# Item records loaded and added inside the aggregation stage, in four column chunks

## The chip, the cores and the metric

The kernel runs on one core of one Trainium2 chip. Its engines are TensorE (PE, matrix products), VectorE (DVE), ScalarE (ACT), GpSimd (POOL) and SyncE (SP), beside 16 DMA engines. Each engine has its own instruction stream; streams meet only at semaphores. The metric is the time of one execution on the device, in microseconds.

## The reference, cut to what matters

Four layers run one after the other over a graph of 6250 nodes with 256 features and 200,000 edges. The first is a weighted aggregation; it is the one that the change touches:

```
y   = layernorm(x)
x   = x + segment_sum(edge_weight[:, None] * y[dst], src)     # 200,000 edges
x   = x + experts(layernorm(x))
x   = x + graph_attention(layernorm(x), src, dst)
x   = x + lstm_layer(layernorm(x))                            # 6250 steps
```

## The kernel before

The nodes are cut into 49 blocks of 128. The edges are sorted by the block of their source node into "items": one item is a column of 128 edges that all belong to one block, and two neighbouring items always belong to the same block. There is room for 1664 items. The stages run one behind the other; each is a block of the program that every engine must leave before the next one starts:

- **stage_scatter** (L161) computes a place for every edge and writes a record of three floats (source, destination, weight; 12 bytes) with one indirect DMA for each 128 edges into tables in device memory. There are five such tables (`WAYS`), so that five scatters can be under way; a place holds its record in one table and zeros in the other four. The stage also stores the normalised rows y in device memory, and makes `BW` (the block of each item).
- **stage_items** (L430) loads the five tables, 128 partitions by 1664 items by 3 floats each, adds them up on VectorE, and takes the sum apart into `DST` (the node to gather, an integer), `EW` (the weight) and `LO` (the source's position in its block). `BI` holds the block number of each pair of items.
- **stage_aggregate** (L491) has 104 turns of 16 items. ScalarE copies a half turn's eight columns of `DST` to `ag_idx`; GpSimd issues one indirect DMA per item that gathers 128 rows of y (1 KB each); VectorE makes a 128x128 matrix per item ("pick": the weight where a column number equals `LO`, else zero); TensorE multiplies pick by rows and sums each pair of items; VectorE adds the pair's sum to its block of `X`. There is one set of 16 row buffers. Four of them are refilled together: in turn i GpSimd waits, ahead of its gathers 4q to 4q+3, until the pairs 2q and 2q+1 of turn i-1 have been summed (`summed`), and for the index copy (`staged`).
- then the experts, the attention (which uses `DST`, `LO` and `EW` again) and the LSTM, each behind the one before.

Constants: P = 128, NI = 1664, U = 16, UP = 8, RF = 3, WAYS = 5, TURNS = 104. On VectorE, `link(...)` issues an instruction and then waits for its end.

Of the kernel before, what the change touches and what calls it, by code (L numbers as in the profile page):

```python
# [16 lines left out]
ALU = mybir.AluOpType  # L17
# [4 lines left out]
P = 128  # L22
# [3 lines left out]
NB = -(-N // P)  # L26
# [11 lines left out]
U = 16  # L38
# [3 lines left out]
UP = U // 2  # L42
NI = -(-((E - NB) // (2 * P) + NB) // UP) * U
TURNS = NI // U
RF = 3
SU = 20
WAYS = 5
# [19 lines left out]
def pair_blocks(nc, g, engine, i, k0, n):  # L67

    return nc.values_load_multi_w_load_instructions(
        g["BI"][0:1, ds(i * UP + k0, n)], [engine], min_val=0, max_val=NB,  # L70
        skip_runtime_bounds_check_because="a number of blocks counted on the chip, at most NB")[1]
# [356 lines left out]


def stage_items(nc, sb, sem, g):  # L430
    part = [sb(f"rec_part{k}", [P, NI * RF]) for k in range(WAYS)]
    loaded, step = sem("rec_loaded"), sem("items_step")
    with nc.Block() as block:
        @block.sync
        def _(sp):
            for k in range(WAYS):
                sp.dma_start(part[k][:, :], g["rec"][k].rearrange("(p r) f -> p (r f)", p=P)).then_inc(loaded, 16)

        @block.vector
        def _(dve):  # L440
            n = [0]

            def link(ins):
                n[0] += 1
                ins.then_inc(step, 1)
                dve.wait_ge(step, n[0])

            dve.wait_ge(loaded, 16 * WAYS)

            for k in range(1, WAYS):  # L450
                link(nc.vector.tensor_tensor(part[0][:, :], part[0][:, :], part[k][:, :], ALU.add))
            rec = part[0][:, :].rearrange("p (r f) -> p r f", f=RF)
            link(nc.vector.tensor_copy(g["DST"][:, 0:NI], rec[:, :, 1]))
            link(nc.vector.tensor_copy(g["EW"][:, 0:NI], rec[:, :, 2]))

            link(nc.vector.tensor_scalar(part[1][:, 0:NI], g["BW"][:, :], float(P), 1.0, ALU.mult, ALU.add))
            link(nc.vector.tensor_tensor(g["LO"][:, 0:NI], rec[:, :, 0], part[1][:, 0:NI], ALU.subtract))

            link(nc.vector.tensor_copy(g["BI"][0:1, 0:NI // 2], g["BW"][0:1, 0:NI:2]))

            link(nc.vector.memset(g["BI"][0:1, NI // 2:NI // 2 + UP], NB))
            link(nc.vector.memset(g["DST"][:, NI:NI + U], 0))
            link(nc.vector.memset(g["LO"][:, NI:NI + U], -1.0))
            link(nc.vector.memset(g["EW"][:, NI:NI + U], 0.0))


def gather_rows(pool, nc, g, table, rows, idx, staged, summed):

    with pool.Fori(0, TURNS) as i:
        for q in range(GPT):  # L470
            if q % 2 == 0:
                pool.wait_ge(staged, i * 2 + (q // 2 + 1))
            pool.wait_ge(summed, i * UP + 2 * (q + 1))
            own_wait(pool, g)
            for u in range(q * GU, (q + 1) * GU):
                pool.indirect_dma_start(rows[:, u, :], None, table,  # L476
                                        bass.IndirectOffsetOnAxis(ap=idx[:, u // HU, u % HU:u % HU + 1], axis=0)).then_inc(g["got"][q], 16)


def stage_indices(nc, g, idx, i, h, staged):  # L480
    nc.scalar.copy(idx[:, h, :], g["DST"][:, ds(i * U + h * HU, HU)]).then_inc(staged, 1)
# [9 lines left out]
def stage_aggregate(nc, sb, sem, g):  # L491
    idx = sb("ag_idx", [P, 2, HU], I32)
    rows = sb("ag_rows", [P, U, D])
    pick = sb("ag_pick", [P, U, P])
    free = sb("ag_free", [1, 2])
    sums = [g["ps"][k][:, 0:D] for k in range(UP)]
    staged, picked, summed, added = (sem(n) for n in ("ag_staged", "ag_picked", "ag_summed", "ag_added"))
    with nc.Block() as block:
        @block.scalar
        def _(act):  # L500
            for h in range(2):
                stage_indices(nc, g, idx, 0, h, staged)
            with act.Fori(0, TURNS) as i:
                for h in range(2):
                    for q in (2 * h, 2 * h + 1):
                        act.wait_ge(g["got"][q], i * (16 * GU) + 16 * GU)
                    stage_indices(nc, g, idx, i + 1, h, staged)

        @block.gpsimd
        def _(pool):  # L510
            pool.memset(free[:, 0:1], 0.0).then_inc(summed, UP)
            gather_rows(pool, nc, g, g["y"], rows, idx, staged, summed)

        @block.tensor
        def _(pe):
            with pe.Fori(0, TURNS) as i:
                for k in range(UP):
                    pe.wait_ge(picked, i * UP + (k + 1))
                    pe.wait_ge(added, i * UP + (k + 1))
                    if k % 2 == 0:  # L520
                        pe.wait_ge(g["got"][k // 2], i * (16 * GU) + 16 * GU)
                    for u in (2 * k, 2 * k + 1):
                        m = nc.tensor.matmul(sums[k], pick[:, u, :], rows[:, u, :], start=u == 2 * k, stop=u == 2 * k + 1)  # L523
                    m.then_inc(summed, 1)

        @block.vector
        def _(dve):
            def picks(i, h):
                dve.wait_ge(summed, i * UP + (h + 1) * (UP // 2))
                for u in range(h * HU, (h + 1) * HU):  # L530
                    m = nc.vector.tensor_scalar(pick[:, u, :], g["iota"][:, :], g["LO"][:, ds(i * U + u, 1)], g["EW"][:, ds(i * U + u, 1)],
                                                ALU.is_equal, ALU.mult)
                    if u % 2 == 1:
                        m.then_inc(picked, 1)

            def adds(i, h):
                blocks = pair_blocks(nc, g, mybir.EngineType.DVE, i, h * UP // 2, UP // 2)
                for n, b in enumerate(blocks):
                    k = h * UP // 2 + n
                    dve.wait_ge(summed, i * UP + (UP + k + 1))  # L540
                    dve.wait_ge(added, i * UP + (UP + k))
                    nc.vector.tensor_tensor(g["X"][:, ds(b, 1), :], g["X"][:, ds(b, 1), :], sums[k], ALU.add).then_inc(added, 1)

            nc.vector.memset(free[:, 1:2], 0.0).then_inc(added, UP)
            picks(0, 0)
            with dve.Fori(0, TURNS) as i:
                picks(i, 1)
                adds(i, 0)
                picks(i + 1, 0)
                adds(i, 1)  # L550
# [1164 lines left out]
def build(nc, ins, out):  # L1715
    with ExitStack() as ctx:
# [24 lines left out]
        with ExitStack() as items:  # L1741
            kept = lambda name, shape, dt=F32: items.enter_context(nc.sbuf_tensor(name, shape, dt))
            g["BW"] = kept("item_block", [P, NI])
            g["BI"] = kept("pair_block", [1, NI // 2 + UP], I32)
            with ExitStack() as recs:
                g["REC"] = recs.enter_context(nc.sbuf_tensor("records", [EP, EC, RF], F32))
                g["POS"] = recs.enter_context(nc.sbuf_tensor("places", [EP, EC], I32))
                stage(stage_places)
                stage(stage_scatter)
            g["DST"] = kept("item_dst", [P, NI + U], I32)  # L1750
            g["LO"] = kept("item_lo", [P, NI + U])
            g["EW"] = kept("item_weight", [P, NI + U])
            stage(stage_items)
            stage(stage_aggregate)
            stage(stage_experts)
            g["AS"] = kept("alpha_src_and_max", [P, NB + 1, 2 * HEADS])
            stage(stage_heads)
            g["NUM"] = kept("numerators", [P, NB + 1, D + HEADS])
            with ExitStack() as scores:
                g["ADE"] = scores.enter_context(nc.sbuf_tensor("item_alpha_dst", [P, NI + U, HEADS], F32))  # L1760
                stage(stage_maxima)
                stage(stage_attend)
            stage(stage_project)
# [16 lines left out]
```

## Time and profile before

| | us |
|---|---|
| median of 3 runs (22097.25 to 22099.84) | 22098.49 |
| profiled execution, its time | 22100.69 |
| profiled execution, span of the trace | 22099.0 |
| last scatter of stage_scatter starts | 2162.64 |
| loads of stage_items are issued from | 2168.74 |
| first gather of stage_aggregate | 2231.95 |
| last gather of stage_aggregate starts | 4340.13 |
| next stage (experts) begins | about 4361 |

Times in the trace count from the start of the span. The span runs from the first to the last instruction, so it is 1.7 us short of the execution's own time. The work around the change fills 0.06 ms of 22 ms; about three fifths of the span are the LSTM's.

### The profile page before, as it was taken

The page shows a single profiled execution, that of the slowest core. Times are in us where ns is not written, and L with a number is a line of the kernel's source. Part 1 is how long each engine was busy: PE and PEld are TensorE (multiplying, and loading weights), DVE is VectorE, ACT ScalarE, POOL GpSimd, SP SyncE. Part 2 cuts the span into 40 slices and gives each one's busy share as a digit, 9 for nine tenths or more (in the row PEclk, how much of TensorE's full clock was granted, in tenths as well). Part 3 has the DMA queues.
Part 4 walks back from the last instruction along what each step waited for, and adds up shares of the span by engine and source line. Part 5 has one row for each costly group of instructions (what it writes and reads, how often), then busy time and mean ns, then how long its engine had stood idle before and what let it go on. Part 6 is the DMA issues. An engine that isn't in the chain of part 4 may idle for free. (4 is left out here: it accounts for less than half of the span.)

```text
span 22099.0 us, 1508424 instructions
## 1 busy us (share of the span) xinstructions
PE 17428.3 (79%) x637604; PEld 12607.9 (57%) x637604; DVE 11072.8 (50%) x43264; ACT 7724.9 (35%) x35209; POOL 6178.2 (28%) x11376
## 2 busy tenths in 40 slices
PE   0000555577888888999999999999999999999998
PEld 0000333355666665666666666666666666666665
DVE  6500333336666666555555555555555555555555
ACT  1000000025555553444444444444444444444443
POOL 6776777605444442000000000000000000000000
PEclk9999777787777778999999999999999999999999
DMA  1001333402222223000000000000000000000000
GB/s 40 1 1 36 99 104 104 88 12 68 63 64 64 64 64 82 2 2 2 2 2 2 2 2 2 2 2 2 2 2 2 2 2 2 2 2 2 2 2 13
DMA packets 334772, 559.74 MB, mean 25 GB/s; under 512 B 141918, under 2 KB 219138, under 8 KB 333314
## 3 DMA queue, kind: packets, MB, share of 16 engines
q0 software_dynamic: 210480, 460.22, 7.8%
q1 hardware_dynamic: 124242, 98.95, 1.4%
q8 instruction: 19, 0.31, 0.0%
q14 instruction: 31, 0.25, 0.0%
HBM read 498.35 MB, written 60.37 MB: 25 GB/s over the span
## 5 line engine op out<-in xcount | busy, mean ns | idle before, releaser
L1468 PE MATMUL banks<-ls_wake 128*1 128x512 bf16 x65000 | 5779.7, 379 | 0.0
L1462 POOL TENSOR_TENSOR ls_d<-ls_sf,ls_cell 128x2 f32<-128x2 f32 x6250 | 1256.1, 201 | 11880.2 <-ACT ls_sf L1523 11880.2
L1507 PE MATMUL banks<-ls_w,ls_ht 128*2 128x64 f32 x200000 | 3937.2, 219 | 1.2 <-issue 1.2
L523 PE MATMUL banks<-ag_rows,ag_pick 128*128 128x256 f32 x3328 | 1207.9, 527 | 3080.6 <-DMA ag_rows<-y_table,ag_idx 3053.9
L1523 ACT ACTIVATE ls_sf<-ls_f_cols 128x2 f32<-128x2 f32 x6250 | 1278.3, 205 | 5636.3 <-DVE ls_f_cols L1559 5636.3
L1559 DVE STREAM_TRANSPOSE ls_f_cols<-banks 128x64 f32<-128x64 f32 x6250 | 1559.8, 250 | 3289.3 <-PE banks L1501 3289.3
L1507 PEld LDWEIGHTS banks<-ls_w,ls_ht 128*2 128x2 f32 x200000 | 3099.5, 85 | 1.3 <-issue 1.3
L523 PEld LDWEIGHTS banks<-ag_rows,ag_pick 128*128 128x128 f32 x3328 | 836.4, 263 | 3451.5 <-DMA ag_rows<-y_table,ag_idx 2432.9
L1501 PE MATMUL banks<-ls_w,ls_ht 128*1 128x64 f32 x100000 | 2525.5, 218 | 323.8 <-issue 0.5
L1501 PEld LDWEIGHTS banks<-ls_w,ls_ht 128*1 128x1 f32 x100000 | 1352.4, 82 | 2295.4 <-DVE ls_ht L1571 2294.7
L1512 PE MATMUL banks<-ls_w,ls_ht 128*1 128x64 f32 x100000 | 2541.3, 219 | 1.0 <-issue 1.0
L998 POOL DMA_INDIRECT at_rows<-row_table,at_idx x1664 | 1659.6, 997 | 1869.5 <-ACT at_idx L1010 1399.8
L1561 DVE STREAM_TRANSPOSE ls_ig_cols<-banks 128x64 f32<-128x64 f32 x6250 | 1558.4, 249 | 1235.0 <-PE banks L1507 1235.0
L1480 PE MATMUL banks<-ls_xp,ls_sel 128*1 128x64 f32 x50000 | 1840.2, 219 | 261.3 <-DVE ls_ig_cols L1561 249.9
L1571 DVE SCALAR_TENSOR_TENSOR ls_ht<-ls_to,ls_tc 128x2 f32<-128x2 f32 x6250 | 1015.9, 163 | 1692.7 <-ACT ls_tc L1530 1692.7
L1491 PE MATMUL banks<-ls_xp,ls_sel 128*1 128x64 f32 x50000 | 1844.0, 219 | 0.0
L1485 PE MATMUL banks<-ls_xp,ls_sel 128*2 128x64 f32 x50000 | 1834.4, 218 | 0.0
L1525 ACT ACTIVATE ls_d<-ls_ig_cols 128x4 f32<-128x4 f32 x6250 | 1302.7, 208 | 1515.3 <-DVE ls_ig_cols L1561 1515.3
L259 POOL DMA_INDIRECT rec_table<-st_rec,st_idx x1560 | 1586.4, 1017 | 548.0 <-issue 472.4
L476 POOL DMA_INDIRECT ag_rows<-y_table,ag_idx x1664 | 1594.7, 958 | 515.6 <-issue 495.3
L1512 PEld LDWEIGHTS banks<-ls_w,ls_ht 128*1 128x1 f32 x100000 | 1697.3, 84 | 1.2 <-issue 1.2
L1468 PEld LDWEIGHTS banks<-ls_wake 128*1 128x1 bf16 x65000 | 1684.4, 84 | 0.0
(324 smaller groups left out, 22962.4 us busy)
## 6 DMA issues: line engine op xcount, KB each, us to landing
ag_rows<-y_table,ag_idx POOLq DMA_INDIRECT x1664
at_rows<-row_table,at_idx POOLq DMA_INDIRECT x1664
projections<-xp_out SPq DMA_DIRECT2D x49, 512.0 KB, 2.6
rec_table<-st_rec,st_idx POOLq DMA_INDIRECT x1563, 2.1
ls_xp<-projections SPq DMA_DIRECT2D x1250, 12.0 KB
ls_xp<-projections SPq DMA_DIRECT2D x1250, 8.0 KB, 1.5
rec_table<-zero POOLq DMA_DIRECT2D x5, 2496.0 KB, 18.3
rec_part<-rec_table SPq DMA_DIRECT2D x5, 2496.0 KB, 19.9
```

The lines of the kernel that those rows point to most:

```text
L259: pool.indirect_dma_start(g["rec"][k], bass.IndirectOffsetOnAxis(ap=idx[:, h, u % SH:u % SH + 1], axis=0), recs[:, h, u % SH, :], None).th ...
L476: pool.indirect_dma_start(rows[:, u, :], None, table, bass.IndirectOffsetOnAxis(ap=idx[:, u // HU, u % HU:u % HU + 1], axis=0)).then_inc(g ...
L523: m = nc.tensor.matmul(sums[k], pick[:, u, :], rows[:, u, :], start=u == 2 * k, stop=u == 2 * k + 1)
L998: pool.indirect_dma_start(rows[:, r, u, :], None, g["rows"], bass.IndirectOffsetOnAxis(ap=idx[:, r, u:u + 1], axis=0)).then_inc(g["got"][r ...
L1468: nc.tensor.matmul(bank_wake[32 * j:32 * j + 1, :], wake[:, 0:1], wake[:, :], start=True, stop=True, tile_position=(0, 32 * j))
L1480: nc.tensor.matmul(bank_f[32 * j:32 * j + 1, 0:HD], sel[:, u, j, 0:1], xp[:, b, HD:2 * HD], start=True, stop=False, tile_position=(0, 32 * j))
L1485: nc.tensor.matmul(bank_ig[32 * j:32 * j + 2, 0:HD], sel[:, u, j, :], xp[:, b, 0:HD], start=True, stop=False, tile_position=(0, 32 * j))
L1491: x = nc.tensor.matmul(bank_o[32 * j:32 * j + 1, 0:HD], sel[:, u, j, 1:2], xp[:, b, HD:2 * HD], start=True, stop=False, tile_position=(0, ...
L1501: m = nc.tensor.matmul(bank_f[32 * j:32 * j + 1, 0:HD], ht[:, v, c, 1:2], w[:, c, j, HD:2 * HD], start=False, stop=c == 1, tile_position=( ...
L1507: m = nc.tensor.matmul(bank_ig[32 * j:32 * j + 2, 0:HD], ht[:, v, c, 1 - r:3 - r], w[:, c, j, lo:lo + HD], start=False, stop=(r, c) == (1, ...
L1512: m = nc.tensor.matmul(bank_o[32 * j:32 * j + 1, 0:HD], ht[:, v, c, 1:2], w[:, c, j, 3 * HD:4 * HD], start=False, stop=c == 1, tile_positi ...
L1559: vec.transpose(f_cols[:, :], bank_f[:, 0:HD]).then_inc(turned, 1)
```

## The change

stage_items is emptied. Its loads and its arithmetic move into stage_aggregate, cut into `COLS` = 4 chunks of `CI` = 416 items:

- SP issues 20 loads instead of 5: for each chunk the same 416 columns of all five tables, 128 rows of 4,992 bytes each, with one semaphore per chunk. The tiles have the same bytes as before; their shape is written with three dimensions.
- VectorE first scales `BW` (now into `EW`, which serves as scratch for it) and makes `BI`, then for each chunk waits for its five loads, does the four additions, the copy to `DST` (which raises `known`), the subtraction to `LO` and the copy to `EW`. The padding of the three tiles comes last; that of `DST` raises `known` a fifth time. Only behind all this stand the picks of turn 0 and the loop.
- ScalarE waits for `known` 1 before the index copies of turn 0, and for `known` 5 before its loop, which copies the indices of turn 1 and later.

GpSimd's and TensorE's programs are the same as before.

```diff
--- before.py
+++ after.py
@@ -428,40 +428,9 @@
 
 
 def stage_items(nc, sb, sem, g):
-    part = [sb(f"rec_part{k}", [P, NI * RF]) for k in range(WAYS)]
-    loaded, step = sem("rec_loaded"), sem("items_step")
-    with nc.Block() as block:
-        @block.sync
-        def _(sp):
-            for k in range(WAYS):
-                sp.dma_start(part[k][:, :], g["rec"][k].rearrange("(p r) f -> p (r f)", p=P)).then_inc(loaded, 16)
-
-        @block.vector
-        def _(dve):
-            n = [0]
-
-            def link(ins):
-                n[0] += 1
-                ins.then_inc(step, 1)
-                dve.wait_ge(step, n[0])
-
-            dve.wait_ge(loaded, 16 * WAYS)
-
-            for k in range(1, WAYS):
-                link(nc.vector.tensor_tensor(part[0][:, :], part[0][:, :], part[k][:, :], ALU.add))
-            rec = part[0][:, :].rearrange("p (r f) -> p r f", f=RF)
-            link(nc.vector.tensor_copy(g["DST"][:, 0:NI], rec[:, :, 1]))
-            link(nc.vector.tensor_copy(g["EW"][:, 0:NI], rec[:, :, 2]))
-
-            link(nc.vector.tensor_scalar(part[1][:, 0:NI], g["BW"][:, :], float(P), 1.0, ALU.mult, ALU.add))
-            link(nc.vector.tensor_tensor(g["LO"][:, 0:NI], rec[:, :, 0], part[1][:, 0:NI], ALU.subtract))
-
-            link(nc.vector.tensor_copy(g["BI"][0:1, 0:NI // 2], g["BW"][0:1, 0:NI:2]))
-
-            link(nc.vector.memset(g["BI"][0:1, NI // 2:NI // 2 + UP], NB))
-            link(nc.vector.memset(g["DST"][:, NI:NI + U], 0))
-            link(nc.vector.memset(g["LO"][:, NI:NI + U], -1.0))
-            link(nc.vector.memset(g["EW"][:, NI:NI + U], 0.0))
+
+    g["columns"] = 4
+
 
 
 def gather_rows(pool, nc, g, table, rows, idx, staged, summed):
@@ -493,13 +462,25 @@
     rows = sb("ag_rows", [P, U, D])
     pick = sb("ag_pick", [P, U, P])
     free = sb("ag_free", [1, 2])
+    COLS = g["columns"]
+    CI = NI // COLS
+    part = [sb(f"rec_part{k}", [P, NI, RF]) for k in range(WAYS)]
+    loaded, step, known = [sem(f"rec_loaded{c}") for c in range(COLS)], sem("items_step"), sem("items_known")
     sums = [g["ps"][k][:, 0:D] for k in range(UP)]
     staged, picked, summed, added = (sem(n) for n in ("ag_staged", "ag_picked", "ag_summed", "ag_added"))
     with nc.Block() as block:
+        @block.sync
+        def _(sp):
+            for c in range(COLS):
+                for k in range(WAYS):
+                    sp.dma_start(part[k][:, c * CI:(c + 1) * CI, :], g["rec"][k].rearrange("(p r) f -> p r f", p=P)[:, c * CI:(c + 1) * CI, :]).then_inc(loaded[c], 16)
+
         @block.scalar
         def _(act):
+            act.wait_ge(known, 1)
             for h in range(2):
                 stage_indices(nc, g, idx, 0, h, staged)
+            act.wait_ge(known, COLS + 1)
             with act.Fori(0, TURNS) as i:
                 for h in range(2):
                     for q in (2 * h, 2 * h + 1):
@@ -541,7 +522,28 @@
                     dve.wait_ge(added, i * UP + (UP + k))
                     nc.vector.tensor_tensor(g["X"][:, ds(b, 1), :], g["X"][:, ds(b, 1), :], sums[k], ALU.add).then_inc(added, 1)
 
+            n = [0]
+
+            def link(ins):
+                n[0] += 1
+                ins.then_inc(step, 1)
+                dve.wait_ge(step, n[0])
+
             nc.vector.memset(free[:, 1:2], 0.0).then_inc(added, UP)
+            link(nc.vector.tensor_scalar(g["EW"][:, 0:NI], g["BW"][:, :], float(P), 1.0, ALU.mult, ALU.add))
+            link(nc.vector.tensor_copy(g["BI"][0:1, 0:NI // 2], g["BW"][0:1, 0:NI:2]))
+            link(nc.vector.memset(g["BI"][0:1, NI // 2:NI // 2 + UP], NB))
+            for c in range(COLS):
+                cols = slice(c * CI, (c + 1) * CI)
+                dve.wait_ge(loaded[c], 16 * WAYS)
+                for k in range(1, WAYS):
+                    link(nc.vector.tensor_tensor(part[0][:, cols, :], part[0][:, cols, :], part[k][:, cols, :], ALU.add))
+                nc.vector.tensor_copy(g["DST"][:, cols], part[0][:, cols, 1]).then_inc(known, 1)
+                link(nc.vector.tensor_tensor(g["LO"][:, cols], part[0][:, cols, 0], g["EW"][:, cols], ALU.subtract))
+                link(nc.vector.tensor_copy(g["EW"][:, cols], part[0][:, cols, 2]))
+            nc.vector.memset(g["DST"][:, NI:NI + U], 0).then_inc(known, 1)
+            link(nc.vector.memset(g["LO"][:, NI:NI + U], -1.0))
+            link(nc.vector.memset(g["EW"][:, NI:NI + U], 0.0))
             picks(0, 0)
             with dve.Fori(0, TURNS) as i:
                 picks(i, 1)
```

## Rows read from the trace of the kernel before

**Rows 1.** Busy time by stretch: stretch, its length, engines, PEclk, DMA share, GB/s.

```profile
2184.00:2188.00 4.00, 0.00 (x0) 0.00 (x0) 0.00 (x0) 0.00 (x0) 0.00 (x0) 1.00 1.00 429
2500.00:3900.00 1400.00, 800.02 (x2216) 553.44 (x2216) 523.06 (x1666) 27.25 (x138) 1062.46 (x1109) 0.76 0.35 104
4300.00:4340.00 40.00, 20.97 (x48) 15.07 (x48) 11.17 (x36) 0.59 (x3) 24.38 (x26) 0.74 0.95 78
```

**Rows 2.** Timeline, 2160 to 2253 us: start, length, engine, line, operation, idle before.

```profile
2162.64 0.91 POOL L266 DMA_INDIRECT rec_table<-st_rec,st_idx  x1 [0.30 <-issue]
2168.74 2.41 SPq L437 DMA_DIRECT2D rec_part<-rec_table  x5
2201.44 21.54 DVE L451 TENSOR_TENSOR rec_part<-rec_part 128x4992 f32<-128x4992 f32 x4 [453.12 <-DMA rec_part<-rec_table]
2223.01 1.27 DVE L453 CAST item_dst<-rec_part 128x1664 int32<-128x1664 f32 x1
...
2225.62 1.03 DVE L456 TENSOR_SCALAR rec_part<-item_block 128x1664 f32<-128x1664 f32 x1
2226.68 2.37 DVE L457 TENSOR_TENSOR item_lo<-rec_part 128x1664 f32<-128x1664 f32 x1
2229.09 0.58 DVE L459 CAST pair_block<-item_block 1x832 int32<-1x832 f32 x1
...
2230.74 0.30 ACT L481 COPY ag_idx<-item_dst 128x8 int32<-128x8 int32 x2 [82.17 <-PEq L433]
...
2230.85 4.26 DVE L531 TENSOR_SCALAR ag_pick<-iota,item_lo,item_weight 128x128 f32<-128x128 f32 x16
2231.95 1.01 POOL L476 DMA_INDIRECT ag_rows<-y_table,ag_idx  x1 [1.14 <-ACT ag_idx L481]
...
2238.58 3.78 PE L523 MATMUL banks<-ag_rows,ag_pick 128*128 128x256 f32 x8 [2167.45 <-DMA ag_rows<-y_table,ag_idx]
...
2242.51 0.42 DVE L542 TENSOR_TENSOR X<-X,banks 128x256 f32 x1 [1.28 <-PE banks L523]
...
2252.25 0.96 POOL L476 DMA_INDIRECT ag_rows<-y_table,ag_idx  x1 [0.30 <-issue]
```

**Rows 3.** All gathers of L476: duration ns min/median/max, and idle before them.

```profile
L476 POOL DMA_INDIRECT ag_rows<-y_table,ag_idx x1664: 950/957/1077, 2231.9 to 4340.1; - x185
...
  issue: 495.3, 1626
```

**Rows 4.** All instructions on the tile rec_part: the loads, and their landing.

```profile
L437 SPq DMA_DIRECT2D rec_part<-rec_table x5: 349/426/543, 2168.7 to 2170.7; - x5
...
DMA to landing us min/median/max: 8.9/19.9/30.8
```

**Rows 5.** Shorter VectorE additions (L542, L1215): duration ns min/median/max.

```profile
L542 DVE TENSOR_TENSOR X<-X,banks x832: 404/421/423, 2240.8 to 4359.7; 128x256 f32 x167
...
L1215 DVE TENSOR_TENSOR at_msg<-at_rows,at_msg x104: 679/681/684, 5080.0 to 8589.5; 128x512 f32<-128x512 f32 x104
```

**Rows 6.** Busy time by stretch, columns as in group 1.

```profile
4.00:10.00 6.00, 0.00 (x0) 0.00 (x0) 0.00 (x0) 0.00 (x0) 5.82 (x9) 1.00 0.93 349
2000.00:2100.00 100.00, 0.00 (x0) 0.00 (x0) 0.00 (x0) 2.78 (x16) 76.16 (x79) 1.00 0.02 1
```

**Rows 7.** Timeline where indirect DMAs meet VectorE operations with two SBUF inputs.

```profile
800.98 1.95 DVE L392 SCALAR_TENSOR_TENSOR item_block<-item,cum,item_block 128x1664 f32<-128x1664 f32 x1 [0.41 <-DVE item_block L392]
801.72 2.05 POOL L259 DMA_INDIRECT rec_table<-st_rec,st_idx  x1 [0.30 <-issue]
803.33 1.95 DVE L392 SCALAR_TENSOR_TENSOR item_block<-item,cum,item_block 128x1664 f32<-128x1664 f32 x1 [0.41 <-DVE item_block L392]
...
5080.03 0.68 DVE L1215 TENSOR_TENSOR at_msg<-at_rows,at_msg 128x512 f32<-128x512 f32 x1
...
5080.55 1.00 POOL L998 DMA_INDIRECT at_rows<-row_table,at_idx  x1 [0.30 <-issue]
5080.63 0.42 DVE L1223 TENSOR_TENSOR numerators<-numerators,at_fade 128x260 f32 x1
```

## The prediction

> **What bounds the kernel now.** I first looked at the busy times of the page and at its slices, to see how much work can be touched at all, then at the timeline between the last scatter and the second turn of the aggregation, then at the lines of the gathers and of the loads. The reader should see three things.
>
> First, the stretch from 2168.74 to 2231.95 us, 63.2 us, is one serial chain [rows 2]. SP issues five loads; VectorE, idle until then, starts its additions at 2201.44; four additions take 21.54 us, and the copies, the scaling, the subtraction and `BI` follow until about 2230.2; then a stage border, the index copy at 2230.74, and the first gather at 2231.95. Nothing else runs beside it. The loads run at full rate: 429 GB/s at a DMA share of 1.00 [rows 1].
>
> Second, the aggregation is bound by GpSimd's issue of gathers. 1664 of them take 957 ns in the median, and nearly all of the idle time before them (495.3 us, 0.30 us for each) ended by "issue", that is by nothing that the trace shows to be waited for [rows 3]. One gather costs 1.27 us and a turn of 16 costs 20.3 (2231.95 to 2252.25) [rows 2]. TensorE is busy 57% and VectorE 37% of a middle stretch, DMA 0.35 at 104 GB/s [rows 1]. In the last turns the DMA engines bind (0.95 at 78 GB/s) [rows 1]; those turns also hang on the turn before, so they move with the rest. So an earlier gather 17, the first of turn 1, is an earlier end of the stage by the same amount, provided that GpSimd then runs on without a pause. The next stages begin only behind this one.
>
> Third, therefore the right quantity is the start of gather 17, now 2252.25 us, and not that of gather 1: turn 0 has its row buffers free and needs only `known` 1, but turn 1 needs turn 0 summed, and for that the picks, which need all four chunks.
>
> **The change, step by step.** The last scatter, the border behind it and SP's first issue stay: 2168.7 us.
>
> *The load of a chunk.* A table's load was 2.556 MB. The first landed 8.9 us after its issue and the last, issued at 2170.7, after 30.8 [rows 4], so at 2201.5. At 429 GB/s 2.556 MB are 5.96 us, which leaves 3.0 us ahead of the first. A chunk is a quarter of each of the five tables, 5 x 0.639 = 3.195 MB, 7.45 us at 429. Its pieces are 4,992 bytes instead of 19,968, and the trace has no such load. The nearest row is the load of the edges in pieces of 6,248 bytes, 349 GB/s [rows 6]. I take 400, between the two, because that row also holds the start and the end of its transfers: 8.0 us a chunk, bounds 7.45 and 9.15. Twenty issues at 0.48 us (2.41 for five) [rows 2] end 9.7 us after the first and hold nothing up. So chunk 0 is there at 2168.7 + 3.0 + 8.0 = 2179.7.
>
> *VectorE's work on a chunk.* L1215 takes 681 ns for 512 columns and L542 421 ns for 256 [rows 5]; from 512 to 4992 columns (5.36 us [rows 2]) the slope is 1.044 ns, so about 0.15 us of each instruction is fixed. Four additions of 1248 columns: 4 x (0.15 + 1.30) and 0.16 of gaps, 5.96 us. `DST` costs (1.27 - 0.15) / 4 + 0.15 = 0.43 and `EW`, the same copy of a column in three, as much, `LO` (2.37 - 0.15) / 4 + 0.15 = 0.71 [rows 2]; with the gaps 7.6 us a chunk, 30.4 in all, against 26.4 for the same work before (21.54 + 2 x 1.27 + 2.37). The scaling of `BW` and the copy to `BI`, 1.03 and 0.58 us [rows 2], now lie ahead of the wait for chunk 0, hidden by its load; without that cover they would cost 1.6.
>
> *Gather 1.* 2179.7 + 6.0 + 0.45 = 2186.2 for `known` 1. From the index copy to the gather it was 1.2 us (2230.74 to 2231.95) [rows 2]: 2187.4, which is 44.5 us earlier than before. Turn 0 ends 20.3 us later, at 2207.7.
>
> *The chunks behind it.* Chunk 1 lands at 2187.7 and is done at 2195.3. Chunks 2 and 3 share the DMA engines with the gathers of turn 0. By bytes the gathers take 104 of 429 GB/s, a quarter; by their DMA share they take 0.35 [rows 1]. I take the bytes, since shares of two queues may overlap. Chunk 2 lands at 2188.5 + 7.2 / 0.76 = 2198.0 and is done at 2205.6; chunk 3 lands at 2208.5 and is done at 2216.1. So the load and not VectorE ends last.
>
> *Gather 17.* Behind chunk 3 stand the padding (0.3), the first two picks (4.26 / 16 each, 0.5) [rows 2], and two pairs on TensorE: from 2238.58 to VectorE's addition at 2242.51 it was 3.9 us [rows 2]. With 0.3 for the semaphores gather 17 starts 5.0 us behind 2216.1, at 2221.1. The index copy of turn 1, queued on ScalarE behind `known` 5, is ready some 3 us earlier. The wait for `known` 5 thus costs nothing of its own: ScalarE has nothing else, and the picks hold turn 1 longer. After it, the next pairs take 3.8 us for two [rows 2], GpSimd 5.1 for four gathers, so it doesn't pause again.
>
> *Sum.* 2252.25 - 2221.1 = 31 us less. The border between the two stages (0.6 us) is in it. Against the profiled execution's own 22100.7 us that gives 22069.7; against the median, which is 2.2 us lower, 22067.5.
>
> *A lock that the trace shows.* While VectorE runs an operation with two SBUF inputs, an indirect DMA of GpSimd does not end: beside additions of 1.95 us (L392) it takes 2.05 us instead of 0.96, and it ends 0.84 us behind each of them; the same at 5080.55, where L1215 ends at 5080.71 and the DMA at 5081.55 [rows 7]. The change puts twelve such additions (chunks 1 to 3) beside turn 0. One gather for each addition makes 1.49 us a gather, at most 24 us for turn 0, which then ends at 2211, still ahead of gather 17. I cost it at nothing, with the ten microseconds until 2221 as the cover. The Trainium skill has this as a rule (SBUF - State Buffer, "Who interferes with whom": whichever of the two starts first holds the shared port pair for its whole instruction); by the rows it holds here, though the page infers that `tensor_tensor` spares the making of descriptors, and by that turn 0 would end at 2207.7: the sum is 31 us either way.
>
> **The rivals.**
>
> *VectorE is the bound.* If the gathers take nothing from the loads, chunk 3 lands at 2203.7 and VectorE ends at 2179.7 + 30.4 = 2210.1; gather 17 at 2215.1, 37 us less, 22061. At 429 GB/s as well 22060.5. For it: gathers are small beside the loads. Against: the loads already fill the DMA engines (share 1.00) [rows 1].
>
> *Slow loads.* With 349 GB/s [rows 6] and 0.35 of the engines lost to gathers, chunk 0 lands at 2180.9, chunk 2 at 2204.0, chunk 3 at 2214.8; gather 17 at 2227.5, 25 us less, 22074.
>
> *The lock holds through all additions.* If GpSimd gets in only between chunks and not between additions, turn 0 grows by 3 x 6.0 us and ends at 2225.6: 27 us less, 22072. Against it: the DMA at 5080.55 was let in at 5080.71 although the next operation with two SBUF inputs stood directly behind (5080.63) [rows 7].
>
> *Every load pays its start.* If the 20 loads ran one behind the other with 3.0 us each, a chunk would take 5 x 4.5 = 22.3 us and chunk 3 would land near 2258; gather 17 at 2271, 18 us more, 22117. Against it: the five loads now landed 5.9 us apart, all of it transfer [rows 4]. The Trainium skill speaks for a part of it (DMA: Bandwidth & Descriptors, "Rules for kernel authors": at least 1 MiB for each DMA for full rate; the loads shrink from 2.4 to 0.6 MiB); its figure of 341 GB/s at 1 MB gives about what "Slow loads" gives from rows.
>
> *The loads fall into records; this is the other side.* The tile and the table are now written with the record's 3 floats as a dimension of their own. If the transfer is cut along it, it has 1.06 million pieces of 12 bytes instead of 2,560. The scatters move such pieces: 79 of them, 10,112 pieces, for a share of 0.02 of 16 engines over 100 us [rows 6], 3.2 ns of an engine a piece. That makes 213 us for the loads instead of 32, so chunk 3 comes some 175 us later: 22098 - 31 + 175, about 22243, and several times as much if a piece costs more from device memory. The change is slower as soon as the load takes 31 us more than I think. Against it: in each row the columns of a chunk are contiguous on both sides, and the whole-table transfer was not cut.
>
> **How the numbers follow.** My forecast of 31 us, with the load as the last to end, has 0.50; VectorE as the bound 0.22; slow loads 0.10; the lock through all additions 0.05; a start for every load 0.03; records 0.05; something that I don't see 0.05. The likeliest time is 22067.5. The range for 8 in 10 takes in the first four cases with 2 to 4 us at either end for the fixed costs: 22057 to 22080. A measurement tells this kernel from no change at about 0.2%, 44 us. The gain can't pass that: gather 17 can't start before turn 0's 16 gathers are issued, 44.5 us earlier than now, and VectorE's 30.4 us keep it 7 us behind that. So faster by over 0.2% has 0.04 (a part of what I don't see, above all a later stage that runs otherwise), within 0.2% 0.89, slower 0.07 (the records, and 0.02 of what I don't see).
>
> **What the changed profile would show.** SP issues 20 loads from about 2168.7; the first addition starts at 2179.7; gather 1 at 2187 and gather 17 at 2221; between them gathers that end 0.84 us behind an addition; VectorE idle before the additions of chunks 2 and 3 with the load as releaser; the experts 31 us earlier, all later stages shifted by the same. The prediction is wrong if gather 17 is released by something else than TensorE, if the number of packets of SP's queue grows by far more than 2,160, or if a later stage lasts otherwise than before.

## The result and the profile after

| | before | changed |
|---|---|---|
| median of 22 runs, us | 22098.47 (22094.49 to 22101.55) | 22068.14 (22062.24 to 22072.14) |
| ratio of the changed kernel to before, 95% interval | | 0.9986 [0.998, 0.9992] |
| span of the profiled execution, us | 22099.0 | 22066.8 |

The change takes 30.3 us off, 0.14%; 31 had been forecast, at 22067.5 us. All 22 runs of one kernel lie apart from all 22 of the other. One of the ten runs of e6_psum_adds below took 32339.5 us at a mean granted clock of 0.618, where all other runs in this text have 0.915 to 0.928, and it is left out.

The page of the changed kernel gives the span, SP's queue (packets, MB, share of the DMA engines) and the gathers of the aggregation (now L445; busy, mean ns, idle before):

```profile
span 22066.8 us, 1508142 instructions
...
q1 hardware_dynamic: 126402, 98.96, 1.4%
...
L445 POOL DMA_INDIRECT ag_rows<-y_table,ag_idx x1664 | 1599.9, 961 | 539.1 <-issue 498.7
```

SP's queue had 124,242 packets before. It has 2,160 more, which is 15 more transfers of 144 packets each: the chunks' rows are moved whole, and the 3 floats of a record were not cut apart.

The timeline of the changed kernel over the same stretch as [rows 2]:

```profile
2161.97 0.91 POOL L266 DMA_INDIRECT rec_table<-st_rec,st_idx  x1 [0.30 <-issue]
2168.06 16.77 SPq L476 DMA_DIRECT2D rec_part<-rec_table  x20
...
2168.14 1.03 DVE L533 TENSOR_SCALAR item_weight<-item_block 128x1664 f32<-128x1664 f32 x1
...
2178.55 5.93 DVE L540 TENSOR_TENSOR rec_part<-rec_part 128x1248 f32<-128x1248 f32 x4 [8.64 <-DMA rec_part<-rec_table]
2184.52 0.44 DVE L541 CAST item_dst<-rec_part 128x416 int32<-128x416 f32 x1
...
2184.99 0.30 ACT L450 COPY ag_idx<-item_dst 128x8 int32<-128x8 int32 x2 [37.08 <-DVE item_dst L541]
...
2186.10 5.93 DVE L540 TENSOR_TENSOR rec_part<-rec_part 128x1248 f32<-128x1248 f32 x4
2186.20 2.24 POOL L445 DMA_INDIRECT ag_rows<-y_table,ag_idx  x1 [18.04 <-ACT ag_idx L450]
2188.75 1.14 POOL L445 DMA_INDIRECT ag_rows<-y_table,ag_idx  x1 [0.30 <-issue]
...
2194.43 0.96 POOL L445 DMA_INDIRECT ag_rows<-y_table,ag_idx  x1 [0.30 <-issue]
2194.75 5.93 DVE L540 TENSOR_TENSOR rec_part<-rec_part 128x1248 f32<-128x1248 f32 x4 [1.11 <-DMA rec_part<-rec_table]
...
2205.11 5.93 DVE L540 TENSOR_TENSOR rec_part<-rec_part 128x1248 f32<-128x1248 f32 x4 [2.82 <-DMA rec_part<-rec_table]
...
2209.19 1.19 POOL L445 DMA_INDIRECT ag_rows<-y_table,ag_idx  x1 [0.30 <-issue]
2211.07 0.44 DVE L541 CAST item_dst<-rec_part 128x416 int32<-128x416 f32 x1
...
2212.16 0.43 DVE L543 COPY item_weight<-rec_part 128x416 f32<-128x416 f32 x1
2212.66 0.07 DVE L544 MEMSET item_dst<- 128x16 int32 x1
...
2212.94 4.19 DVE L512 TENSOR_SCALAR ag_pick<-iota,item_lo,item_weight 128x128 f32<-128x128 f32 x16
2213.07 0.38 ACT L450 COPY ag_idx<-item_dst 128x8 int32 x2 [27.79 <-DVE item_dst L544]
...
2213.68 9.80 PE L504 MATMUL banks<-ag_rows,ag_pick 128*128 128x256 f32 x32 [2142.54 <-DVE ag_pick L512]
...
2218.26 0.95 POOL L445 DMA_INDIRECT ag_rows<-y_table,ag_idx  x1 [7.89 <-PE banks L504]
...
2219.52 0.95 POOL L445 DMA_INDIRECT ag_rows<-y_table,ag_idx  x1 [0.30 <-issue]
```

What the reader is to see: SP issues 20 loads from 2168.06. VectorE's first additions start at 2178.55, not at 2201.44. ScalarE copies the first indices at 2184.99, and gather 1 starts at 2186.20 instead of 2231.95 [rows 2]. The additions of chunks 2 and 3 stand behind a wait for their loads (1.11 and 2.82 us). GpSimd has issued the 16 gathers of turn 0 by 2210.38 and then waits 7.89 us for TensorE, whose wait ended with the picks (L512), which in turn stand behind the last chunk. Gather 17 starts at 2218.26; before it started at 2252.25, without a wait [rows 2].

The loads beside nothing and beside gathers, by stretch (columns as in [rows 1]), and the loads and their landing:

```profile
2172.00:2184.00 12.00, 0.00 (x0) 0.00 (x0) 5.35 (x4) 0.00 (x0) 0.00 (x0) 1.00 1.02 416
2188.00:2204.00 16.00, 0.00 (x0) 0.00 (x0) 12.86 (x13) 0.00 (x0) 12.65 (x12) 1.00 1.02 401
```

```profile
L476 SPq DMA_DIRECT2D rec_part<-rec_table x20: 350/487/3072, 2168.1 to 2183.5; - x20
...
DMA to landing us min/median/max: 4.1/13.8/21.5
```

All 16 DMA engines stay full in both stretches. SP's issues grow to 3.07 us at most, but the last load is issued at 2183.5, 21 us ahead of its landing, so the issue holds nothing up.

**Where the time went.** The executions place the whole stretch differently: SP's first load is at 2168.7 us before and at 2168.1 and 2165.4 in two executions of the changed kernel. In the rest of the text I count from that issue. Gather 17 stands at 83.5 us before and at 50.2 now, 33.3 less; the next stage begins (first load of the experts) at 2192.1 before and 2159.1 now, 33.1 less; the spans differ by 32.2 and the medians by 30.3. So the stage passes its gain on whole.

### The profile page after: what moved, and what is told of

It is laid out like the page before. It is cut to its first block and busy times, and to the rows that moved or that the text cites. A ratio compares the mean times of both kernels' runs of the same rounds, so it can differ in the third digit from the quotient of the medians.

```text
span 22066.8 us, 1508142 instructions
## 1 busy us (share of the span) xinstructions
PE 17362.8 (79%) x637293; PEld 12587.0 (57%) x637604; DVE 11073.9 (50%) x43285; ACT 7726.5 (35%) x35209; POOL 6175.0 (28%) x11376
## 5 line engine op out<-in xcount | busy, mean ns | idle before, releaser
L445 POOL DMA_INDIRECT ag_rows<-y_table,ag_idx x1664 | 1599.9, 961 | 539.1 <-issue 498.7
```

Of the source, the lines that this page charges most:

```text
L445: pool.indirect_dma_start(rows[:, u, :], None, table, bass.IndirectOffsetOnAxis(ap=idx[:, u // HU, u % HU:u % HU + 1], axis=0)).then_inc(g ...
```

## The experiments

Two groups of four ran on one chip each, and each kernel is compared with the kernel before on the same chip (median 22092.91 us in the first group, 22097.29 in the second). All columns but the last count from SP's first load in the profiled execution; the last is the median of before less that of the kernel, with the ratio's 95% interval.

| kernel | gather 1 | gather 17 | experts begin | less than before |
|---|---|---|---|---|
| before | 63.2 | 83.5 | 2192.1 | |
| changed, 22 runs | 18.1 | 50.2 | 2159.1 | 30.3 [0.998, 0.9992] |
| e1_gathers_last | 42.4 | 62.6 | 2167.2 | 19.7 [0.9983, 1.0001] |
| e2_early_picks | 18.0 | 41.3 | 2148.0 | 41.4 [0.9973, 0.9991] |
| e3_one_chunk | 56.9 | 78.7 | 2183.8 | 6.4 [0.9988, 1.0006] |
| e4_eight_chunks | 11.9 | 50.3 | 2156.9 | 30.0 [0.9978, 0.9996] |
| e5_two_chunks | 30.9 | 58.4 | 2161.8 | 26.7 [0.9979, 0.9997] |
| e6_psum_adds | 18.0 | 50.1 | 2155.3 | 31.1 [0.9976, 0.9996] |
| e7_interleaved | 6.3 | 29.9 | 2137.4 | 49.9 [0.9968, 0.9986] |
| e8_changed_again | 17.9 | 50.0 | 2155.5 | 30.8 [0.9977, 0.9995] |

The intervals of the two groups are about 0.09% wide to each side, 20 us, so e1 and e3 can't be told from the kernel before by them alone. What tells these kernels apart is the place of gather 17 in the trace: how much earlier than before's it is agrees with the last column to within 4 us in every row.

### e1_gathers_last: the loads and VectorE overlap, the gathers don't

```diff
-            act.wait_ge(known, 1)
+            act.wait_ge(known, COLS + 1)
             for h in range(2):
                 stage_indices(nc, g, idx, 0, h, staged)
```

> Four chunks as in the changed kernel, but ScalarE waits for all chunks before it copies the indices of turn 0, so no gather runs beside loads or chunk work. Theory (the first gather of turn 1, gather 17, sets the end; loads are slowed by gathers): without gathers beside them the loads no longer hold VectorE up, its chunk work ends at about 2209.2 (2178.5 + 4 x 7.56 + 0.4) instead of 2212.9, gather 1 starts at 2210.5 and gather 17 20.3 us later at 2230.8, 12.5 us behind the changed kernel's 2218.3: about 22080.5. Rival (the gain is all from overlapping loads with VectorE, turn 0 is no part of it): no change from 22068.

Measured: gather 17 12.6 us behind e8's, 19.7 us less than before instead of 18 forecast. The rival falls: the gathers of turn 0 are part of the gain. The timeline shows the additions of chunks 2 and 3, the padding of `DST` and gather 1:

```profile
2190.68 5.94 DVE L540 TENSOR_TENSOR rec_part<-rec_part 128x1248 f32<-128x1248 f32 x4 [0.39 <-DMA rec_part<-rec_table]
...
2198.21 5.93 DVE L540 TENSOR_TENSOR rec_part<-rec_part 128x1248 f32<-128x1248 f32 x4
...
2205.77 0.07 DVE L544 MEMSET item_dst<- 128x16 int32 x1
...
2207.09 1.01 POOL L445 DMA_INDIRECT ag_rows<-y_table,ag_idx  x1 [42.24 <-ACT ag_idx L450]
```

SP's first issue is at 2164.74 here. Behind chunk 0 only chunk 2 is waited for (0.39 us), 25.9 us behind that issue, and chunk 3 is there in time: VectorE sets the end of the chunk work. With gathers beside it (changed kernel) the last additions began 37.1 us behind the issue, here 33.5: the gathers beside the loads cost 3.6 us, where the expectation had 3.7.

### e2_early_picks: turn 0's picks behind chunk 0

```diff
             for c in range(COLS):
...
                 link(nc.vector.tensor_copy(g["EW"][:, cols], part[0][:, cols, 2]))
+                if c == 0:
+                    picks(0, 0)
+                    picks(0, 1)
...
-            picks(0, 0)
-            with dve.Fori(0, TURNS) as i:
+            adds(0, 0)
+            picks(1, 0)
+            adds(0, 1)
+            with dve.Fori(1, TURNS) as i:
                 picks(i, 1)
```

ScalarE copies the indices of turn 1 ahead of its wait for all chunks, too.

> The picks of turn 0 stand directly behind chunk 0, and ScalarE copies the indices of turn 1 before it waits for all chunks. Theory: gather 17 is then released by gather 16 and not by TensorE behind the last chunk; turn 0 takes about 24 us from 2186.2 because of the lock, so gather 17 starts at 2210.5, 8 us earlier than in the changed kernel: about 22060. Rival A (something other than the picks behind the last chunk holds gather 17, or GpSimd pauses at turn 2 instead): 22068. Rival B (without the lock turn 0 would take 20.3 us): gather 17 at 2206.8, 22056.5.

Measured: gather 17 stands at 41.3 us, 8.7 earlier than in e8 (8 forecast), and the median is 41.4 us under before's. The timeline shows the picks, the first matrix products, gathers 16 and 17 and the end of the chunk work:

```profile
2183.55 4.32 DVE L516 TENSOR_SCALAR ag_pick<-iota,item_lo,item_weight 128x128 f32<-128x128 f32 x16
...
2193.47 3.78 PE L508 MATMUL banks<-ag_rows,ag_pick 128*128 128x256 f32 x8 [2122.04 <-DMA ag_rows<-y_table,ag_idx]
...
2205.52 1.19 POOL L445 DMA_INDIRECT ag_rows<-y_table,ag_idx  x1 [0.30 <-issue]
2207.01 1.19 POOL L445 DMA_INDIRECT ag_rows<-y_table,ag_idx  x1 [0.30 <-issue]
...
2210.53 0.07 DVE L551 MEMSET item_dst<- 128x16 int32 x1
```

TensorE begins while VectorE still adds chunks; gather 17 follows gather 16 after 0.30 us, released by nothing but the issue, ahead of the last chunk's end. This undoes the wait of 7.89 us of the changed kernel and gives back its price, so gather 17 sets the end, and what held it stood behind the last chunk. Rival A falls. The edit lifts two waits at once, though: that for the picks and that of ScalarE for all chunks. In the changed kernel the index copy of turn 1 starts at 2213.07, and a gather starts 1.2 us behind its index copy; so without the picks' wait gather 17 could have started at about 2214.3 (an estimate) instead of 2218.26. The picks thus hold it 4.0 us longer than ScalarE does; moving them alone was not tried. Rival B had 38.7 us for gather 17 and the lock theory 42.4; with 41.3 B falls. The first four gathers now run beside picks and take 0.96 to 1.01 us, but most of the others still meet additions (1.18 to 1.54). The group ran on another chip than e8, so the comparison of the two goes over before's medians.

### e3_one_chunk, e5_two_chunks, e4_eight_chunks: the number of chunks

The edit of e3; e5 has 2 and e4 has 8 in its place.

```diff
-    g["columns"] = 4
+    g["columns"] = 1
```

> One chunk: the items made inside the aggregation without being cut. Theory: last load lands at 2200.9, four additions 21.5 us and the copy to DST 1.3, gather 1 at 2225.1, turn 0 20.3 us, the picks ready before it needs them: gather 17 at 2245.4, 6.2 us less than before (the border, the scaling of BW, and LO and EW under turn 0): 22092.5. Rival (moving the work into the stage is worth nothing by itself): 22098. Rival (the move is worth most of the 30 us): 22070.

> Two chunks of 832 items. Theory: chunk 0 lands at 2186.5, gather 1 at 2199.7, chunk 1 lands about 2203 with 13.9 us of work behind it, D 2217, gather 17 at 2222.6, 4.3 us more than the changed kernel: 22072.5. Rival (four chunks are no better than two, the gain is the overlap as such): 22068.

> Eight chunks of 208 items, loads of 0.3 MB. Theory: VectorE's work grows to 8 x 4.35 = 34.8 us but starts at 2174.7; loads land last at about 2206 with only 4.4 us of work behind them: D about 2210.5, gather 17 at 2216.3, 2 us less than the changed kernel: 22066, hardly to be told from it. Rival (small loads lose rate, or every load pays its start): 22075 or more.

Measured: 6.4, 26.7 and 30.0 us less than before, with 6.2, 26 and 32.5 forecast. Moving the work into the stage is worth a fifth of the gain (6.4 us by the medians, 4.8 by gather 17), the first cut about 20 us, the second 4, the third nothing. Eight chunks start gather 1 5.9 us earlier than e8, and all of it ends in a longer wait for TensorE. Additions of the last chunk and gather 17, with eight chunks:

```profile
2206.31 3.33 DVE L540 TENSOR_TENSOR rec_part<-rec_part 128x624 f32<-128x624 f32 x4 [0.48 <-DMA rec_part<-rec_table]
...
2216.03 0.95 POOL L445 DMA_INDIRECT ag_rows<-y_table,ag_idx  x1 [14.48 <-PE banks L504]
```

Behind the last landing there is less work than with four chunks, as forecast, but the last landing itself is later: 40.6 us after SP's first issue, 37.1 with four. The traces give most of that to the small loads: alone, from 3.9 to 11.9 us behind the first issue, they run at 387 GB/s, and those of e8 at 414 in the same stretch, by which the 12.8 MB would take some 2 us longer (an estimate). My forecast for gather 17 was 48.2, measured 50.3.

Two chunks met their time, but not by the forecast path. Gather 17 of e5 stands at 58.4 us instead of 54.5, and not TensorE releases it but the issue of gather 16:

```profile
2222.69 0.95 POOL L445 DMA_INDIRECT ag_rows<-y_table,ag_idx  x1 [0.30 <-issue]
```

Its turn 0 takes 27.5 us instead of 20.3, since its gathers meet additions of 2.78 us (rows under e6). VectorE's chunk work ends 46.7 us behind the first issue; with the 5.7 us that gather 17 stands behind it in the changed kernel, the picks would have let it start at 52.4 (an estimate). So here the lock costs about 6 us, and much of what the second cut gives (8.4 us by gather 17, 4 by the medians) is that the additions beside the gathers get shorter.

### e6_psum_adds: whose lock is it

```diff
-                for k in range(1, WAYS):
-                    link(nc.vector.tensor_tensor(part[0][:, cols, :], part[0][:, cols, :], part[k][:, cols, :], ALU.add))
+                acc = g["banks"][:, 0:3, 0:CI]
+                link(nc.vector.tensor_tensor(acc, way(0), way(1), ALU.add))
+                link(nc.vector.tensor_tensor(acc, acc, way(2), ALU.add))
+                link(nc.vector.tensor_tensor(acc, acc, way(3), ALU.add))
+                link(nc.vector.tensor_tensor(way(0), acc, way(4), ALU.add))
```

`way(k)` is the same chunk of table k, written as three rows of 416.

> Of the four additions of a chunk the first has both inputs in SBUF; the other three take one input from PSUM, where the sum is kept. Lock theory: only the first addition of a chunk holds a gather back; the others leave gathers at 0.96 us, turn 0 ends about 2 us earlier, and gather 17 stays where it is (2218), since it waits for TensorE: about 22068. Rival (gathers of turn 0 are long because their queue shares the DMA engines with the loads): they stay at 1.14 to 1.19 us beside all additions.

The timeline of e6 beside the additions of chunk 2: the first adds two SBUF tiles into PSUM, the next two add an SBUF tile to PSUM, and the fourth writes such a sum back to SBUF:

```profile
2192.01 1.47 DVE L541 TENSOR_TENSOR banks<-rec_part 128x1248 f32<-128x1248 f32 x1 [1.30 <-DMA rec_part<-rec_table]
2192.62 1.67 POOL L445 DMA_INDIRECT ag_rows<-y_table,ag_idx  x1 [0.30 <-issue]
2193.51 1.47 DVE L542 TENSOR_TENSOR banks<-banks,rec_part 128x1248 f32<-128x1248 f32 x1
2194.60 0.95 POOL L445 DMA_INDIRECT ag_rows<-y_table,ag_idx  x1 [0.30 <-issue]
2195.01 1.47 DVE L543 TENSOR_TENSOR banks<-banks,rec_part 128x1248 f32<-128x1248 f32 x1
2195.86 0.95 POOL L445 DMA_INDIRECT ag_rows<-y_table,ag_idx  x1 [0.30 <-issue]
2196.51 1.46 DVE L544 TENSOR_TENSOR rec_part<-banks,rec_part 128x1248 f32<-128x1248 f32 x1
2197.12 0.95 POOL L445 DMA_INDIRECT ag_rows<-y_table,ag_idx  x1 [0.30 <-issue]
```

The additions take as long as in the changed kernel (1.47 us against 1.46). The gather that starts inside the first one takes 1.67 us and ends at 2194.29, 0.81 behind its end; the gathers beside the other three take 0.95. So the two inputs in SBUF count, and not where the result goes. Loads and other traffic are the same, so a queue shared with the loads is not what lengthens the gathers. Turn 0's last gather starts 39.5 us after the first load, in e8 at 40.9: 1.4 us earlier, 2 forecast. Gather 17 doesn't move (50.1 and 50.0), nor does the time. e5 varies the length of the additions; three rows, the additions of 2.78 us and two gathers beside them:

```profile
2197.13 11.14 DVE L540 TENSOR_TENSOR rec_part<-rec_part 128x2496 f32<-128x2496 f32 x4 [1.15 <-DMA rec_part<-rec_table]
...
2201.02 2.49 POOL L445 DMA_INDIRECT ag_rows<-y_table,ag_idx  x1 [0.30 <-issue]
2203.81 2.49 POOL L445 DMA_INDIRECT ag_rows<-y_table,ag_idx  x1 [0.30 <-issue]
```

A gather takes 2.49 us there, one for each addition, and 0.30 between them: the period is the addition's. The last load has landed by then (the DMA share from 2198 to 2208 is 0.19), so no load lengthens these gathers.

### e7_interleaved: a small first chunk, turns placed between the chunks

```diff
-    COLS = g["columns"]
-    CI = NI // COLS
+    SIZES = (32, 384, 416, 416, 416)
...
+            chunk(0); picks(0, 0); picks(0, 1)
+            chunk(1); chunk(2)
+            adds(0, 0); picks(1, 0); adds(0, 1); picks(1, 1)
+            chunk(3)
+            adds(1, 0); picks(2, 0); adds(1, 1); picks(2, 1)
+            chunk(4)
...
+            adds(2, 0); picks(3, 0); adds(2, 1)
+            with dve.Fori(3, TURNS) as i:
```

ScalarE waits for chunk 1 ahead of the indices of turn 2, and for all chunks ahead of those of turn 3.

> Five chunks of 32, 384, 416, 416 and 416 items; the picks and additions of turns 0 to 2 are placed by hand between the chunks, and ScalarE waits for a chunk only before the turn that needs it. Theory: chunk 0 lands at about 2173, gather 1 at 2175.6, 10.6 us earlier than in the changed kernel, and GpSimd never pauses; the lock costs some 4 us over sixteen additions: about 51 us less than before, 22047. Rival (VectorE can't do chunks and turns at once, GpSimd pauses before turn 2 or 3): 22055 to 22062.

Measured: 22047.4 us, 49.9 less than before (51 forecast) and 19.1 less than the changed kernel on the same chip. The additions of the small chunk, gather 1, and gathers 16 and 17:

```profile
2167.97 1.13 DVE L548 TENSOR_TENSOR rec_part<-rec_part 128x96 f32<-128x96 f32 x4 [1.85 <-DMA rec_part<-rec_table]
...
2170.57 1.11 POOL L445 DMA_INDIRECT ag_rows<-y_table,ag_idx  x1 [6.19 <-ACT ag_idx L450]
...
2192.66 1.19 POOL L445 DMA_INDIRECT ag_rows<-y_table,ag_idx  x1 [0.30 <-issue]
...
2194.16 0.95 POOL L445 DMA_INDIRECT ag_rows<-y_table,ag_idx  x1 [0.30 <-issue]
```

SP's first issue is at 2164.27, so gather 1 stands 6.3 us behind it, 11.6 earlier than in e8. Gather 17 follows gather 16 at once, 20.1 us earlier than e8's. Behind gather 1 GpSimd waits for ScalarE eight times, 9.5 us in all, where e8 has 8.0: VectorE keeps up with chunks and turns, and the rival falls. This version beats both kernels. Against e2 it changes two things, the size of the first chunk and the place of turns 1 and 2; what each is worth was not tried.

### e8_changed_again

> The changed kernel once more on the same chip, to compare the others with: 22068, gather 17 at about 2218.

Measured: 22066.54 us, 30.8 less than before on that chip, gather 17 at 50.0. Its span is the same 22066.8 as that of the first profile, but its experts begin 3.6 us earlier behind the first load, and 6.3 us earlier in the span; the stages behind them take all of it back. So a stage's place in a single execution is good only to a few microseconds here. Of the 3 us between gather 17's 33.3 and the medians' 30.3, 1.9 are that the profiled execution of before took 2.2 us more than its median and that of the changed kernel 0.4 more; the last microsecond lies within this scatter.

## Why the prediction was right

*Gather 17 as the quantity.* Right. It moved by 33.3 us, and in nine kernels its place and the time move together. Gather 1 is not the quantity: e4 starts it 5.9 us earlier for nothing, and e1 starts it 24.5 us later for 11.

*What releases it.* Right for the changed kernel: TensorE, behind the picks, behind the last chunk. (With two chunks it is turn 0 itself, see e5.) I had 5.0 us from the end of chunk 3 to gather 17; from 2212.59 to 2218.26 it is 5.7.

*VectorE's work.* Right to 0.1 us: the additions of a chunk take 5.93 us (5.96 forecast), a chunk 7.55 (7.6), an addition of 1248 columns 1457 ns (1.45).

*The loads.* The term that was mis-sized. I had taken 400 GB/s alone and a quarter lost to gathers: first additions of the chunks at 11.0, 19.0, 29.3 and 39.8 us after the first issue. They began at 10.5, 18.0, 26.7 and 37.1. Pieces of 4,992 bytes run at 416 GB/s alone and share 401 with the gathers, so the full rate of [rows 1] was nearer than that of [rows 6]. Between chunks 2 and 3 it is 10.4 us, against 7.7 a chunk in e1 without gathers: 0.26 lost, 0.24 forecast. Up to chunk 2, though, the gathers cost only 0.8 us (16.2 from chunk 0 to chunk 2, twice 7.7 without gathers), with 2.3 forecast. The lock is not the reason, since e6, where it holds 3 gathers up to chunk 3's landing instead of 8, has chunks 2 and 3 at 26.7 and 36.9 us and e8 at 26.6 and 36.8; the reason stays open. All this ended chunk 3 2.9 us earlier than forecast, and gather 17, with the 0.7 lost in the step above, 2.2 us earlier. The median fell 0.7 us short of the forecast all the same. That it came so near is in part luck: by gather 17 alone it would have been 2.3 us beyond the forecast, and the 3 us between trace and medians (see e8) went the other way.

*The lock.* Right in size and in what it cost: a gather that starts inside an addition ends 0.8 to 0.9 us behind it, turn 0's issue ended 42.3 us after the first load (42.3 forecast as the upper end), and it cost nothing, since 7.9 us of waiting stood behind it. e6 shows the cause. The rival that the lock holds through all additions falls: one gather passes between any two. But the words that an indirect DMA does not end while such an operation runs are too wide: the gather of 2194.43 ends at 2195.39, inside the addition that began at 2194.75, and takes its usual 0.96 us. Only gathers that start inside an addition are held. Nor does it work the other way round: that addition starts inside a gather, and all 16 take 1.457 to 1.459 us. So of the rule that the prediction took from the Trainium skill (SBUF - State Buffer, "Who interferes with whom"), that whichever starts first holds the ports, this trace shows only the half in which VectorE starts first. In the same section the Trainium skill infers that `tensor_tensor` spares the making of descriptors; here it doesn't spare an indirect DMA, which was 1.14 to 2.24 us long when it started inside such an addition and 0.96 without.

*The later stages.* From the experts' first load to the end of the span it was 17738.1 us before and 17739.7 now. The 1.5 us more are less than the 6.3 by which two executions of the changed kernel differ there, so the sign named in the prediction (a later stage that lasts otherwise) did not come clear of that scatter.

*The other rivals.* VectorE as the bound is false for the changed kernel (it waited 1.11 and 2.82 us for loads) and true for e1, but for 0.39 us. A start for every load and the cut into records did not come: the chunks landed one behind the other at full rate, in 144 packets for each load. (5 x 4.5 us in the prediction of that rival make 22.5 and not 22.3, which changes nothing.) The Trainium skill's rule for DMA sizes (DMA: Bandwidth & Descriptors, "Rules for kernel authors") asks for 1 MiB; loads of 0.6 MiB, queued one behind the other, kept 97% of the rate of the 2.4 MiB loads (416 of 429 GB/s) here.

## What to carry to other kernels

When a serial stage is folded into the loop that uses its result, look for the first step of the loop that really waits: here it was not the first gather but the seventeenth, which needs the first turn consumed, and the consumer's work stood behind the whole preparation in its engine's program. Cutting finer than that wait helps nothing (four and eight chunks are alike); putting the consumer's first work between the chunks gave another 11 us, and a small first chunk with two more turns between the chunks 8 more. Look at what the early work will meet, too: the loads beside gathers got slower, and so did the gathers that start inside additions with two SBUF inputs. The second costs only where no wait stands behind: nothing with four chunks, about 6 us with two.

## What the runs showed of the hardware

An indirect DMA on GpSimd may be held by more than two-input operations. In e3 gather 1 starts inside the subtraction to `LO` and is followed by the copy to `EW`, which has one SBUF input:

```profile
2222.28 2.39 DVE L542 TENSOR_TENSOR item_lo<-rec_part,item_weight 128x1664 f32<-128x1664 f32 x1
...
2223.61 2.50 POOL L445 DMA_INDIRECT ag_rows<-y_table,ag_idx  x1 [56.83 <-ACT ag_idx L450]
2224.70 1.29 DVE L543 COPY item_weight<-rec_part 128x1664 f32<-128x1664 f32 x1
```

The subtraction ends at 2224.67, but the gather ends at 2226.11, 1.4 us later and 0.1 behind the end of the copy. A gather held by the subtraction alone would have ended some 0.84 us behind it, at about 2225.5. So it looks as if the copy of 1664 columns held it a second time. That was not tried by itself, and the gathers that start beside the copies of 416 columns in the changed kernel (2193.17 and 2201.82) take 0.96 and 0.95 us. Gather 17 of e3 stands 1.5 us later behind gather 1 than the 20.3 us of a turn.

SP's loads were issued faster than they ran only up to a point: with 20 loads a single issue took up to 3.07 us and with 40 up to 2.42, against 0.54 for five [rows 4]. The 20 issues took 16.8 us in all, where the prediction had 9.7. It cost nothing, as the data engines had work the whole time.
